# A transformer block on one core: scatters waited for one by one, two row buffers, roots as Exp of Ln, and several operations at other places

## The reference, cut to what matters

```python
mod = silu(c) @ wmod                      # 8 samples, six parts of 256 columns
sa, ca, ga, sb, cb, gb = parts(mod)       # ga, gb are kept at least 0.25 from zero
h = layernorm(x) * (1 + ca) + sa          # x: 8 x 256 x 256
x = x + ga * attention(h)                 # 16 query heads, 8 key heads of 128, window of 128
h = layernorm(x) * (1 + cb) + sb
x = x + gb * ffn(h)
# attention: qkv = h @ W_pack; rotation of q and k; each key and value row mixed with the one before
#            ("conv"); softmax(q k / sqrt(128)) v; @ W_o
# ffn: xn = rmsnorm(h) * w_norm; top 4 of 32 experts by softmax(xn @ w_router), each expert takes its
#      first 128 rows; silu(row @ w_gate) * (row @ w_up) @ w_down, weighted and added up;
#      plus a shared expert of 704 columns times sigmoid(xn @ w_shared_gate); plus h
```

## Time and profile before

| what | us |
|---|---|
| median of 3 runs | 814.11 (813.59 to 818.44) |
| the profiled execution, run | 815.22 |
| the profiled execution, first to last instruction (span) | 813.0 |
| busy: TensorE, VectorE, ACT, POOL | 754.8, 544.1, 458.0, 427.4 |
| attention, step 0 to the last step's scores | 30.2 to 580 |
| experts | 668 to 751 |

### The profile page before, as it was taken

How to read it: one execution, slowest core, us unless ns; L and a number is a source line. 1 busy time by engine, 2 the same in 40 slices (tenths; PEclk the granted TensorE clock), 3 DMA queues, 4 the chain that set the end, 5 groups by cost and what they waited for, 6 DMA issues and landing times.

```text
span 813.0 us, 12301 instructions
## 1 busy us (share of the span) xinstructions
PE 754.8 (93%) x3858; PEld 621.3 (76%) x3858; DVE 544.1 (67%) x1692; ACT 458.0 (56%) x1148; POOL 427.4 (53%) x337
## 2 busy tenths in 40 slices
PE   4878999999999999899999999999889799998997
PEld 2567888887788888778888878888667567776774
DVE  4578776678877768888686786878454115554265
ACT  4667777777787576778676768776352112221110
POOL 0533435554366388645548855655703605675475
PEclk9999999999999999999999999999898989999999
DMA  8943900000004111100401002040368438997671
GB/s 305 306 100 95 341 1 1 2 0 2 1 1 135 48 38 45 38 1 0 155 2 52 36 21 72 2 156 10 107 173 244 123 110 225 296 296 164 151 250 52
DMA packets 62351, 84.45 MB, mean 104 GB/s; under 512 B 6312, under 2 KB 50229, under 8 KB 62288
## 3 DMA queue, kind: packets, MB, share of 16 engines
q1 hardware_dynamic: 53456, 74.04, 29.0%
q0 software_dynamic: 7680, 8.95, 5.5%
q10 hardware_dynamic: 1152, 0.69, 0.3%
HBM read 54.88 MB, written 33.51 MB: 109 GB/s over the span
## 4 chain that ended last, share of the span: by engine, by line
PE 69%; DVE 14%; ACT 8%; issue 5%; another core or an unknown queue 2%; DMA 2%; SPq 0%; POOL 0%; ACTq 0%; DVEq 0%; POOLq 0%
PE PJ L1269 17%; PE OUT L1367 10%; PE U L1356 5%; PE U L1322 5%; PE U L1518 5%; PE U L1345 4%; PE U L1460 3%; PE OUT L1460 3%; PE U L1321 3%; PE U L1357 3%; ACT U L536 2%; PE U L1269 2%; PE XB L1537 2%; PE OUT L1537 2%
## 5 line engine op out<-in xcount | busy, mean ns | idle before, releaser
L731 POOL TENSOR_TENSOR qsw<-qsw,sinT 128x512 f32<-128x512 f32 x96 | 123.7, 1288 | 222.4 <-ACT qsw L523 221.8
L536 ACT ACTIVATE U<-U,nmax 128x128 f32<-128x128 f32 (+1 forms) x256 | 99.1, 387 | 86.7 <-DVE nmax L928 81.5
L928 DVE CUSTOM_DVE_ANT_0 U<-U,mask 128x128 f32<-128x128 f32 (+1 forms) x256 | 86.8, 380 | 74.7 <-PE U L1322 74.4
L1367 PE MATMUL OUT<-wo,oT 128*128 128x256 f32 x512 | 133.3, 384 | 0.0
L1269 PE MATMUL PJ<-hT_hi,w_hi 128*128 128x512 f32 x256 | 112.1, 438 | 0.8 <-issue 0.8
L1269 PE MATMUL PJ<-hT_lo,w_hi 128*128 128x512 f32 x256 | 101.0, 395 | 0.0
L1269 PE MATMUL PJ<-hT_hi,w_lo 128*128 128x512 f32 x256 | 100.9, 394 | 0.0
L735 POOL TENSOR_TENSOR qr<-qr,qsw 128x512 f32<-128x512 f32 x64 | 82.4, 1288 | 30.0 <-DVE qr L916 26.7
L938 DVE TENSOR_SCALAR prob<-U,rinv 128x128 f32<-128x128 f32 (+1 forms) x256 | 95.1, 413 | 4.5
L1367 PEld LDWEIGHTS OUT<-wo,oT 128*128 128x128 f32 x512 | 88.7, 193 | 6.9
L522 ACT ACTIVATE qsw<-PJ 64x512 f32<-64x512 f32 x96 | 57.0, 593 | 63.3 <-PE PJ L1269 57.8
(11 more groups left out here) (202 smaller groups left out, 1596.9 us busy)
## 6 DMA issues: line engine op xcount, KB each, us to landing
wgu<-in_dram SPq DMA_DIRECT2D x32, 352.0 KB
expert_sum<-blank SPq DMA_DIRECT2D x3, 2176.0 KB, 17.3
wd<-in_dram SPq DMA_DIRECT2D x16, 352.0 KB
slot_rows<-blank SPq DMA_DIRECT2D x1, 4624.0 KB, 24.7
xe<-slot_rows SPq DMA_DIRECT2D x16, 289.0 KB, 4.6
late_sums<-expert_sum SPq DMA_DIRECT2D x9, 512.0 KB, 9.8
wraw<-in_dram SPq DMA_DIRECT2D x8, 512.0 KB, 13.3
bcm<-mod_rows SPq DMA_DIRECT2D x8, 512.0 KB, 6.7
```

What stands on the lines that cost most here:

```text
L536: last = act.activation(U[n % 3][:, a:z], U[n % 3][:, a:z], ACT.Exp, scale=-1.0, bias=nmax[:, n % 4, j:j + 1], accum_out=rsum[:, n % 4, j: ...
L731: pool.tensor_tensor(pair3(qsw[:, n % NQSW, :]), pair3(qsw[:, n % NQSW, :]), both(sinT[:, :]), ALU.mult).then_inc(t2_done, 1)
L928: last = dve.tensor_tensor_reduce(out=U[n % 3][:, a:z], in0=U[n % 3][:, a:z], in1=mask[:, a:z], scale=-float(HD) ** -0.5, scalar=3.4e38, o ...
L1367: last = pe.matmul(OUT[b][:, t * H:(t + 1) * H], oT[:, n % NOT, t * PN:(t + 1) * PN], wo[:, head, :], start=(head == 0 and t == 0), stop=( ...
```

## The change

- **Roots.** Each Sqrt with its reciprocal becomes an Ln with the same scale and bias and an Exp with scale -0.5, both on ACT; the set of tables that holds both is loaded after the first Silu, ahead of the last pair's std and ahead of its RMS root.
- **Places in a pair.** ACT's root for the pair ahead goes from step 5 to 4, the RMS root from 12 to 9; VectorE's normalised rows from 8 and 9 to 5 and 8, `xn` from 13 and 14 to 11 and 12; `k_conv` ahead of the projection.
- **First pair.** Two weight chunks are split ahead of hT and one after it, the others in steps 0, 3, 5, 8 and 13. The modulation rows are made in steps 14 and 17 in the bank `XB`, bounded in 18, 20 and 21; their weights are loaded after W_pack and W_o.
- **Rows.** `xn` has two buffers, so `post_xn` waits for the pair before the last; the wait for the pair before stands ahead of `sidx`.
- **Scatters.** From step 125 on each scatter of pair 2 waits for `ot_done`, then for `sh_ps` (a part of `gate_up(0, ...)`); those of the last pair from the third on wait for `down(0, 3)`, parts of `gate_up(1, ...)`, `down(1, 0)` and `down(1, 1)`.
- **Around the experts.** TensorE's waits ahead of slot 0 stand ahead of slots 1 and 2; the wait for all `ye` stands behind the gate-and-up parts of shared pair 2.
- **End.** Sums are fetched in the order 0, 3, 1, 2; VectorE does the last pair's four operations within `down(2, ...)` and the first two `hidden(3, f)`; ACT issues the stores of the last pair.

```diff
 h2 = sb("h2", [PN, TT, H], F32, att)
-xn = sb("xn", [PN, TT, ROW], F32, att)
+xn = sb("xn", [PN, 2, TT, ROW], F32, att)
...
 mv2 = sb("mv2", [PN, TT, 2], F32, att)
-std2 = sb("std2", [PN, 2, TT], F32, att)
+rstd2 = sb("rstd2", [PN, 2, TT], F32, att)
...
+W_STEPS = (0, 3, 5, 8, 13)
+MOD_STEPS = (14, 17)
+
...
         w_load(j)
-    sp.dma_start(wm[:, :, 2 * H:6 * H], wm_src[:, :, 2 * H:6 * H]).then_inc(ld_wmr, 16)
...
     sp.dma_start(wo[:, :, :], w_o.rearrange("(n p) h -> p n h", p=PN)).then_inc(ld_wo, 16)
+    sp.dma_start(wm[:, :, 2 * H:6 * H], wm_src[:, :, 2 * H:6 * H]).then_inc(ld_wmr, 16)
...
         sp.wait_ge(st_acc[i], 16 * len(range(i, E, NSUM)))
-    for q in range(NPAIR):
+    for q in (0, LAST, 1, 2):
...
             sp.dma_start(sums(q, i), acc_d[i][q * TOK:(q + 1) * TOK, :].rearrange("(t p) h -> p t h", p=PN)).then_inc(ld_sums[q], 16)
-    for q in range(NPAIR):
-        if q < LAST:
-            sp.wait_ge(fin_done[q], 1)
-            sp.dma_start(out[q * TOK:(q + 1) * TOK, :].rearrange("(t p) h -> p t h", p=PN), fin[:, q, :, :]).then_inc(st_out[q % 2], 16)
-        else:
-            for t in range(TT):
-                sp.wait_ge(fin_done[q], t + 1)
-                sp.dma_start(rows(out, q * TOK + t * PN), fin[:, q, t, :]).then_inc(st_out[q % 2], 16)
-    sp.wait_ge(st_out[0], 16 * 2)
-    sp.wait_ge(st_out[1], 16 * (1 + TT))
+    for q in range(LAST):
+        sp.wait_ge(fin_done[q], 1)
+        sp.dma_start(out[q * TOK:(q + 1) * TOK, :].rearrange("(t p) h -> p t h", p=PN), fin[:, q, :, :]).then_inc(st_out[0], 16)
+    sp.wait_ge(st_out[0], 16 * LAST)
+    sp.wait_ge(st_out[1], 16 * TT)
...
     act.activation(sc[:, :], c_sb[:, :], ACT.Silu).then_inc(silu_done, 1)
+    act.preload_act_table_set("natural_log_exp_and_others")
...
         act.wait_ge(var1, 2 * p + 2)
-        act.activation(std1[:, 0, :], mv1[:, :, 1], ACT.Sqrt, bias=LN_EPS).then_inc(std1_done, 1)
+        own(act.activation(rstd1[:, 0, :], mv1[:, :, 1], ACT.Ln, bias=LN_EPS))
+        act.activation(rstd1[:, 1, :], rstd1[:, 0, :], ACT.Exp, scale=-0.5).then_inc(rstd1_done, 1)
...
         act.wait_ge(var2, 2 * p + b1)
-        act.activation(std2[:, 0, 2 * b0:2 * b1], mv2[:, 2 * b0:2 * b1, 1], ACT.Sqrt, bias=LN_EPS).then_inc(std2_done, b1 - b0)
+        own(act.activation(rstd2[:, 0, 2 * b0:2 * b1], mv2[:, 2 * b0:2 * b1, 1], ACT.Ln, bias=LN_EPS))
+        act.activation(rstd2[:, 1, 2 * b0:2 * b1], rstd2[:, 0, 2 * b0:2 * b1], ACT.Exp, scale=-0.5).then_inc(rstd2_done, b1 - b0)
...
     def post_rms(p):
-        act.activation(rms[:, 1, :], rms[:, 0, :], ACT.Sqrt, scale=1.0 / H, bias=RMS_EPS).then_inc(rms_done, 1)
+        own(act.activation(rms[:, 1, :], rms[:, 0, :], ACT.Ln, scale=1.0 / H, bias=RMS_EPS))
+        act.activation(rms[:, 2, :], rms[:, 1, :], ACT.Exp, scale=-0.5).then_inc(rms_done, 1)
...
             return
-        if l == 5:
-            if q < NPAIR:
-                prepare_norm(q)
-            if p >= 0:
-                post_std(p, 0, 2)
+        if l == 4 and q < NPAIR:
+            prepare_norm(q)
+        if l == 5 and p >= 0:
+            post_std(p, 0, 2)
...
                 post_squares(p, l - 7)
-            if l == 12:
+            if l == 9:
...
     prepare_norm(0)
-    for n in range(W_FIRST):
+    for n in range(W_FIRST - 1):
...
         prepare_hi(0, c)
-
-    def mod_rows():
-        act.wait_ge(mod_ps, 2)
-        for j in range(2):
-            last = act.activation(mod[:, j * 2 * H:(j + 1) * 2 * H], OUT[j][0:B, :], ACT.Copy)
-        last.then_inc(rows_done, 1)
+    w_high(W_FIRST - 1)
+
+    def mod_rows(j):
+        act.wait_ge(mod_ps, j + 1)
+        act.activation(mod[:, j * 2 * H:(j + 1) * 2 * H], XB[0:B, :], ACT.Copy).then_inc(rows_done, 1)
...
             k_tap((n + 2) // 4)
-        if 0 <= n < 10 and n % 2 == 0:
-            w_high(W_FIRST + n // 2)
-        if n == 2:
-            mod_rows()
+        if n in W_STEPS:
+            w_high(W_FIRST + W_STEPS.index(n))
+        if n in MOD_STEPS:
+            mod_rows(MOD_STEPS.index(n))
...
     silu_of(0, 2)
+    act.preload_act_table_set("natural_log_exp_and_others")
...
     post_squares(LAST, 1)
+    act.preload_act_table_set("natural_log_exp_and_others")
...
             silu_of(q, f)
+    for t in range(TT):
+        act.wait_ge(fin_done[LAST], t + 1)
+        act.dma_start(rows(out, LAST * TOK + t * PN), fin[:, LAST, t, :]).then_inc(st_out[1], 16)
...
         pool.indirect_dma_start(out=slots_d, out_offset=bass.IndirectOffsetOnAxis(ap=sidx[:, c:c + 1], axis=0),
-                                in_=xn[:, c // TOPK, :], in_offset=None, bounds_check=E * CAP - 1,
+                                in_=xn[:, p % 2, c // TOPK, :], in_offset=None, bounds_check=E * CAP - 1,
...
             if p >= 0:
+                if n >= NU - 3:
+                    pool.wait_ge(ot_done, n - 1)
...
             hooks(n)
-    for l in sorted(SCATTERS):
-        if l >= UNITS:
-            for c in SCATTERS[l]:
-                scatter(LAST - 1, c)
+
+    rest = [c for l in sorted(SCATTERS) if l >= UNITS for c in SCATTERS[l]]
+    for i, c in enumerate(rest):
+        if i < 2:
+            pool.wait_ge(ot_done, NU - 1 + i)
+        else:
+            pool.wait_ge(sh_ps, min(i, FT))
+        scatter(LAST - 1, c)
...
     post_base(LAST, 1)
+
+    PRODUCT = {4: 1, 6: 2, 7: 3, 9: 4, 10: 5, 12: 6}
+    TILE = {2: 0, 13: 1, 15: 2}
     for c in range(TT * TOPK):
+        if c in PRODUCT:
+            pool.wait_ge(sh_ps, FT + PRODUCT[c])
+        if c in TILE:
+            pool.wait_ge(dn_ps, TT + TILE[c])
...
         if b == 0:
-            dve.wait_ge(std1_done, p + 1)
-            own(dve.reciprocal(std1[:, 1, :], std1[:, 0, :]))
+            dve.wait_ge(rstd1_done, p + 1)
         for t in range(2 * b, 2 * b + 2):
-            last = dve.tensor_scalar(xin[:, t, :], xin[:, t, :], mv1[:, t, 0:1], std1[:, 1, t:t + 1],
+            last = dve.tensor_scalar(xin[:, t, :], xin[:, t, :], mv1[:, t, 0:1], rstd1[:, 1, t:t + 1],
...
-        dve.wait_ge(std2_done, 2 * p + (b + 1))
-        own(dve.reciprocal(std2[:, 1, 2 * b:2 * b + 2], std2[:, 0, 2 * b:2 * b + 2]))
+        dve.wait_ge(rstd2_done, 2 * p + (b + 1))
...
         for t in range(2 * b, 2 * b + 2):
-            last = dve.scalar_tensor_tensor(h2[:, t, :], h2[:, t, :], std2[:, 1, t:t + 1], bcm[:, b, H:2 * H],
+            last = dve.scalar_tensor_tensor(h2[:, t, :], h2[:, t, :], rstd2[:, 1, t:t + 1], bcm[:, b, H:2 * H],
...
             dve.wait_ge(rms_done, p + 1)
-            own(dve.reciprocal(rms[:, 2, :], rms[:, 1, :]))
-            if p > 0:
-                dve.wait_ge(st_scat, 16 * TT * TOPK * p)
-            dve.tensor_copy(xn[:, :, TOKEN:TOKEN + 1], token[:, p, :].unsqueeze(2))
+            if p > 1:
+                dve.wait_ge(st_scat, 16 * TT * TOPK * (p - 1))
+            dve.tensor_copy(xn[:, p % 2, :, TOKEN:TOKEN + 1], token[:, p, :].unsqueeze(2))
         for t in range(2 * b, 2 * b + 2):
-            last = dve.scalar_tensor_tensor(xn[:, t, 0:H], h2[:, t, :], rms[:, 2, t:t + 1], wnorm[:, :],
+            last = dve.scalar_tensor_tensor(xn[:, p % 2, t, 0:H], h2[:, t, :], rms[:, 2, t:t + 1], wnorm[:, :],
...
+        if p > 0:
+            dve.wait_ge(st_scat, 16 * TT * TOPK * p)
...
     def first_pair(n):
-        if n % 2 == 1 and n < 10:
-            w_low(W_FIRST + n // 2)
-        if n == 3:
+        if n - 1 in W_STEPS:
+            w_low(W_FIRST + W_STEPS.index(n - 1))
+        if n == 18:
...
             bounded_gate(0)
-        if n == 5:
+        if n == 20:
+            dve.wait_ge(rows_done, 2)
             bounded_gate(3)
-        if n == 7:
+        if n == 21:
...
             own(dve.tensor_scalar(slot_id[:, :], ebase[:, :], 1.0 / CAP, 1.0 - 1.0 / CAP, ALU.mult, ALU.add))
-        if n == 20:
+        if n == 28:
...
                 prepare_stats(q, l // 3)
-            if l in (8, 9):
-                prepare_norm(q, l - 8)
+            if l in (5, 8):
+                prepare_norm(q, (l - 5) // 3)
...
                 post_h2(p, l - 6)
-            if l in (13, 14):
-                post_xn(p, l - 13)
+            if l in (11, 12):
+                post_xn(p, l - 11)
...
     mod_features()
-    for n in range(W_FIRST):
+    for n in range(W_FIRST - 1):
...
         prepare_lo(0, c)
+    w_low(W_FIRST - 1)
...
             head_out(n - 2)
+        if n % 4 == 3 and n + 1 < NU:
+            k_conv((n + 1) // 4)
...
             project(n + 3)
-        if n % 4 == 3 and n + 1 < NU:
-            k_conv((n + 1) // 4)
...
         combine(0, t)
-    for f in range(FT):
-        hidden(3, f)
-        if 1 <= f <= TT:
-            combine(LAST, f - 1)
+        if t >= 2:
+            combine(LAST, t - 2)
+    hidden(LAST, 0)
+    combine(LAST, 2)
+    hidden(LAST, 1)
+    combine(LAST, 3)
+    for f in range(2, FT):
+        hidden(LAST, f)
...
             pe.wait_ge(ht_used, HC * (p + 2))
-        if g == 4 and p > 0:
-            pe.wait_ge(xnt_lo_done, 2 * p - 1)
```

(36 more changed lines are left out.)

10 lines of the change are left out of this document (5 added, 5 removed).

## The result

The changed kernel takes 780.5 us (median of 4 runs, 777.2 to 784.5) against 815.3 (4 runs, 813.6 to 818.4): a ratio of 0.957, with a 95% interval of 0.953 to 0.960. A second measurement, on another chip, gave 785.5 against 817.9, 0.961 (0.958 to 0.965). The forecast was 774, with 766 to 791 as its range (768 to 780 for its main case alone). The profiled execution took 779.9, with a span of 778.1.

What follows compares the result with a forecast made beforehand. The prediction saw TensorE 93% busy, with losses where other engines make it wait or run at the lower clock. Terms summed to 40.6 us off the profiled 815.2, 774.6, given as 774, range 766 to 791.

Steps and rivals of the forecast that it cites:

- First 12 steps: Pair 0's first steps: spacing weight splits and moving modulation rows later gains 7.5 us; their matmuls in steps 14 and 17 cost 3.6.
- Boundaries: Between attention pairs: twelve ACT table loads leave the chain, VectorE is late next, 1.3 us stay lost at each; gain 13 us.
- VectorE is the bound: Rival at the pair boundaries: VectorE's extra work meets POOL, 3.5 us lost each instead of 1.3; 781 us, chance 14%.
- End of attention: From 572 us: pacing POOL's 13 back-to-back scatters removes a 3.1 us hold and 2.9 of lower clock; gain 6 us.
- the last pair's chain: Behind the attention: std's table load comes before its wait, two reciprocals go and two Exps come; gain 1.2 us.
- Last scatters: Shared pair 1 to the experts: pacing the last pair's 16 scatters removes ACT's holds; gain 9.8 us.
- Row buffer: Second row buffer, ahead of post_xn: removes a scatter wait that showed no cost, so no gain was counted.
- Small orders: Around the experts: moving waits ahead of slot 0 (0.6) and of shared pair 2 (0.5) gains 0.9 us.
- Tail: End of kernel: the last pair's sums come earlier and VectorE's additions no longer hold TensorE; gain 3.3 us.
- bursts don't hold anybody: Rival on both scatter bursts: they cause no holds, so 6 + 9.8 us stay lost; 790 us, chance 12%.
- The sets still switch: Rival on the roots: Ln and Exp load tables in turn, six loads a boundary instead of four; 795 us, chance 5%.
- Slower: Rival on pacing: each of some 22 scatters holds work TensorE waits for; 823 us at 1.5 us each, chance 2%.

Runs made afterwards that it cites:

- e1: The changed kernel with the waits taken from the scatters of pair 2 alone, those of the last pair still paced: 796.7 us, ratio 0.977.
- e3: The changed kernel with the two loads of shared pair 3's input issued behind the experts' last loads instead of ahead of the experts: 782.0 us, ratio 0.957.
- e4: The changed kernel with three of the last pair's four additions on VectorE cut into halves of 512 columns, one behind each hidden(3, f): 778.3 us, ratio 0.954.
- e8: The changed kernel with the modulation rows made early, as in the kernel before, weight splits as changed: 785.4 us, ratio 0.962.
- e9: The changed kernel loading only the first quarter of each row of the gate and up weights of experts 8 to 31: 776.2 us, ratio 0.949.
- e7: The changed kernel with the roots as Sqrt and reciprocal again, without the early loads of the table set: 790.2 us, ratio 0.967.
- e2: The changed kernel with the waits taken from the 16 scatters of the last pair alone: 793.2 us, ratio 0.973.
- e5: The kernel before with the scatters' waits of the change and nothing else: 811.3 us, ratio 0.993.
- e6: The kernel before with Sqrt and reciprocal as Ln and Exp, their table set loaded once after the first Silu, no place changed: 813.0 us, ratio 0.994.
- e11: The changed kernel with the last pair's additions in halves and POOL's scatter of step 3 between its two additions to xres: 780.0 us, ratio 0.953.

## Why the prediction was right, and where its terms were off

By its own steps, forecast against the table:

- **Start, 2.5**: 2.0. Right.
- **First 12 steps, 7.5, and the rows' return, -3.6**: 11.0 and -4.0. The mechanism was right, the size short: I kept 2 us of loss, and none is left (47.5, below the pace of 48.1), nor did I count the lower clock that the waits there brought with them. The modulation matmuls of steps 14 and 17 cost 2.0 each where 1.8 were forecast.
- **Boundaries, 13**: 9.1. The table loads were all gained, as said; VectorE late next was said too, with 1.3 of loss at each. Measured by the same sum: 135.9 - 128.2 - 4.8 = 2.9, then 3.0, and 118.2 - 112.1 - 3.9 = 2.2. In pair 1 the loss is 1.4 but for the clock (134.4 in e1, e3, e4, e8 and e9). In pairs 2 and 3 the step that failed is "0.67 of k-convolution": beside POOL's two additions it takes 2.62 and 2.65, and TensorE stands 0.5 us before the next scores, once in each pair. Pair 2 has two more such stands, of 0.5 and 0.6, before 329.4 and 334.6. The 8.1 us lost lie between the forecast's 4 and the 10.5 of the rival "VectorE is the bound", nearer the rival: its mechanism, VectorE meeting POOL, is partly what happened.
- **End of attention, 6, and the last pair's chain, 1.2**: 10.4. Underrated. e1 puts 10.0 on the waits, where I had counted one hold of 3.1 and 2.9 of lower clock; what followed from the hold (more waits, and half clock from 612.4 and 619.2 in the kernel before) was left out. For the chain's own 1.2 that leaves 0.4, and e7 gives 0.7.
- **Last scatters, 9.8**: 10.0. Right, and so is its arithmetic of 27.3 + 0.3; e2 gives 7.2 for the waits alone.
- **Row buffer, 0**: wrong reading. It "showed no cost" because the burst had ended when `xn` was written. Paced, it costs 8.5 (e5). The sum is not touched, since the change has both, but whoever took the pacing without the buffer would have gained 0.7% where the forecast's two terms for it (6 and 9.8) gave 1.9%.
- **Small orders, 0.9**: -5.3 with the experts. This is the term that failed. I took the experts' 83.5 us as fixed, whatever the transfers beside them do. In the kernel before they are nearly all TensorE's (81.1 busy); in the changed one it waits 4.3 for slot rows, and e9 shows 80.4 with fewer bytes. Whether the change or the execution brought these waits stays open, since e6, with the old places, has 4.5 of them.
- **Tail, 3.3**: 1.6. I had two operations of the last pair ahead of POOL's start; one is (744.70, 1.23), the other starts at 747.57, 1 us after POOL, takes 3.43, and TensorE's weight loads wait for `hidden` three times (0.5, 0.7, 0.7).

The terms that were too large (boundaries 3.9, small orders 6.2, tail 1.7, start 0.5) and too small (first steps 3.1 net, end of attention 3.2, last scatters 0.2) leave 40.6 - 34.9 = 5.7, but for rounding. So the mechanisms were mostly right, and the sum is as near as it is in part by luck: 12.3 us of terms too large meet 6.5 too small. The largest miss, the experts', may be chance itself, and the range reached up to 791 for a rival, the bursts that hold nobody, that turned out false; the main case's own range ended at 780.

Of the rivals, "bursts don't hold anybody" falls with e1 and e2. The forecast had named DMA: Bandwidth & Descriptors (Trainium skill), SWDGE vs HWDGE vs iDMA, for it: that the queues take turns in each DMA engine may well be so, but the hold is there, and what is held are instructions of ACT and VectorE whose inputs the trace shows as done, not a transfer of another queue. Where in the chip it arises no run shows. "The sets still switch" falls with the table loads. "Slower" falls: paced scatters hold nobody.

## What to carry to other kernels

Read a resource that "shows no cost" against the order it will have after the change: a buffer, a queue or a load that is idle now may carry the next wait, and the two halves of such a change belong together. Before a stage's time is taken as fixed, look at how busy its transfers are (0.90 of the DMA engines before and 0.96 after, in the experts): with so little room this stage took 83.3 to 92.0 us in profiles with the same loads, and time won elsewhere is blurred by that. Where VectorE and POOL meet on the critical path, count meetings and not columns: put a scatter between POOL's two operations (e11: 1.4 us for the convolution instead of 2.6), rather than cut VectorE's.
